# Last graph stage of a four-layer kernel: unrolled sweeps of unequal width, identity in the diagonal blocks, output rows on ScalarE

## What is computed

```
x = x + gnn0(layernorm(x))        # (adj != 0) @ (h @ W + b) / column sums
x = x + ffn0(layernorm(x))        # 8 experts, the best 2 of each row
x = x + gnn1(layernorm(x), adj)
x = x + ffn1(layernorm(x))

gnn1:  A_t = A + I;  deg = A_t.sum(1);  d = deg ** -0.5
       h = (A_t * d[:, None] * d[None, :]) @ x
       return relu(h @ W.T + b)

ffn1:  hot = x > 0.5 ; decode three one-hot groups of 16 columns (64.., 80.., 96..)
       shift the byte left or right; add 2.0 at a column of 128..143 and one of 144..159
       return x plus that, all 256 columns
```

## Time and profile before

| | us |
|---|---|
| median of 3 runs | 1169.84 |
| the profiled execution | 1168.45 |
| its span | 1166.6 |
| start of the last block | 823.06 |
| first adjacency matmul of the last block | 839.59 |
| last adjacency sum read (start of the last `high_sums`) | 1117.44 |

### The profile page before, as it was taken

How to read it: one execution, slowest core, us unless ns; L and a number is a source line. 1 busy time by engine, 2 the same in 40 slices (tenths; PEclk the granted TensorE clock), 3 DMA queues, 4 the chain that set the end, 5 groups by cost and what they waited for, 6 DMA issues and landing times. The chain is left out here.

```text
span 1166.6 us, 23614 instructions
## 1 busy us (share of the span) xinstructions
PE 985.5 (84%) x6868; PEld 641.1 (55%) x6869; DVE 576.4 (49%) x1661; ACT 388.6 (33%) x792; POOL 345.6 (30%) x359
## 2 busy tenths in 40 slices
PE   5559999999823899999999999995299997997941
PEld 1235544444401699899899899894044443443421
DVE  5633412136699466566566566562561106144077
ACT  3482867676694233233233233231121000000000
POOL 3310000024474254454455454453241001001011
PEclk9879999999955899999999999998599998998976
DMA  9466799899784133232333332232898775776201
GB/s 355 166 214 223 273 325 322 305 329 370 256 274 137 34 51 45 50 51 45 50 50 46 50 52 44 50 52 36 278 419 315 237 265 202 260 244 215 92 29 44
DMA packets 87008, 199.97 MB, mean 171 GB/s; under 512 B 12784, under 2 KB 47088, under 8 KB 86832
## 3 DMA queue, kind: packets, MB, share of 16 engines
q1 hardware_dynamic: 65136, 164.70, 40.5%
q0 software_dynamic: 17648, 30.49, 13.4%
q10 hardware_dynamic: 4176, 4.19, 1.0%
HBM read 176.41 MB, written 22.94 MB: 171 GB/s over the span
## 5 line engine op out<-in xcount | busy, mean ns | idle before, releaser
L955 PE MATMUL bank<-adj_f,feat 128*128 128x512 f16 x1024 | 243.5, 393 | 22.4 <-DMA adj_f<-in_adjT 22.4
L1586 PE MATMUL bank<-adj_g,feat 128*128 128x512 f16 x1024 | 241.0, 393 | 11.3 <-DMA adj_g<-in_adjT 11.3
L1231 ACT ACTIVATE act_f<-bank,b_sb 128x256 f32<-128x256 f32 x304 | 127.4, 470 | 291.9 <-PE bank L1176 291.9
L1176 PE MATMUL bank<-rT,experts 128*128 128x256 f16 x1824 | 208.5, 275 | 3.5 <-DVE rT L1244 3.5
L1197 PE MATMUL bank<-experts,act_h 128*128 x1824 | 205.3, 273 | 1.4 <-DVE y_f L1276 1.4
L1176 PEld LDWEIGHTS bank<-rT,experts 128*128 x1824 | 179.9, 99 | 26.1 <-issue 4.0
L1197 PEld LDWEIGHTS bank<-experts,act_h 128*128 128x128 f16 x1824 | 176.9, 98 | 21.5 <-issue 1.7
L955 PEld LDWEIGHTS bank<-adj_f,feat 128*128 128x128 f16 x1024 | 97.4, 97 | 149.6 <-issue 19.2
L1094 POOL DMA_INDIRECT x_rows<-y,token x76 | 122.1, 1607 | 194.1 <-DVE y L1283 166.4
L1586 PEld LDWEIGHTS bank<-adj_g,feat 128*128 x1024 | 99.1, 97 | 142.9 <-issue 19.4
L837 ACT ACTIVATE spent<-adj_f 128x1024 f16<-128x1024 f32 x128 | 135.1, 1055 | 39.4 <-DMA adj_f<-in_adjT 33.7
(11 more groups left out here) (257 smaller groups left out, 873.5 us busy)
## 6 DMA issues: line engine op xcount, KB each, us to landing
adj_f<-in_adjT SPq DMA_DIRECT2D x128, 512.0 KB, 5.9
adj_g<-in_adjT SPq DMA_DIRECT2D x128, 512.0 KB, 5.0
unit_f<-in_W SPq DMA_DIRECT2D x16, 512.0 KB, 7.1
stage<-in_W SPq DMA_DIRECT2D x12, 512.0 KB, 7.4
x_ring<-in_x POOLq DMA_DIRECT2D x16, 256.0 KB, 7.4
x_rows<-agg SPq DMA_DIRECT2D x4, 1024.0 KB, 10.6
x_sb<-x_rows SPq DMA_DIRECT2D x4, 1024.0 KB, 9.3
agg<-in_x ACTq DMA_DIRECT2D x3, 1024.0 KB, 13.7
```

What stands on the lines that cost most here:

```text
L955: last = pe.matmul(mine(s)[ib * DC + c][:, :], feat0[:, j, h, c * P:(c + 1) * P], adj_0[j % RING][:, ib * HALF_SWEEP:(ib + 1) * HALF_SWEEP ...
L1176: last = pe.matmul(pb[2 + q][:, k * SLOT:(k + 1) * SLOT], w1_part(e * DC + (f // FQ * W2_UNIT0 + c), wh)[:, (f % FQ) * P:(f % FQ + 1) * P] ...
L1231: last = a.activation(act_f[q][:, k, :], pb[2 + q][:, k * SLOT:(k + 1) * SLOT], ACT.Gelu, bias=b1_sb[:, ds(e * FC + (2 * q + k), 1)], scal ...
L1586: last = pe.matmul(mine(s)[ib * DC + c][:, :], feat[:, ds(jg * RING2 + b, 1), h, c * P:(c + 1) * P].rearrange("p a d -> p (a d)"), adj_1[b ...
```

## The change

It rewrites the last block, and adds four transfers to SP's queue in the experts block.

- The output rows are taken in five groups: 8, 8, 8, 4 and 4 row tiles (`GROUPS`), so two sweeps are 512 columns wide. Of those, a tile has 4 matmuls and its load is 256 KB in pieces of 2 KB.
- All loops of the block are unrolled.
- The sums open with `start=` at the first tile. `open_sums`, `add_self` and `eye` are gone. The identity is put into the adjacency tile itself: POOL multiplies the 128 x 128 diagonal block by `grow` (1, and 255 on the diagonal) and adds `ident`, so a diagonal 0 becomes 1 and a 1 becomes 256 (f16 upper half 3.75, twice FLAG).
- `rows_out` of the sweep before stand after tiles 3, 4, 5 ... of a sweep (`ROWS_FROM`).
- The first four adjacency tiles are loaded in the experts block, once DVE has split the last expert weights. The others alternate with the pieces of x, which are now 2, 6, 8, 8 and 8 tiles (`PIECES`).
- The output is made on ACT: `x * (rstd + 1) - mean * rstd` (`make_rows`). DVE makes z for 112 columns alone, and POOL's `add_rest` is gone. The norm's last step writes in place (one copy fewer). Statistics are taken tile by tile in each group.

```
-    w = Region(WORK_AT, X_AT)
+    adj_early = [Region(LATE_AT + k * 4096, W_AT)(f"adj_early{k}", [P, SWEEP], F32) for k in range(EARLY)]
+    GROUPS = ((0, 8), (8, 8), (16, 8), (24, 4), (28, 4))
+    ROWS_FROM = 3
 # experts block, sync
+            sp.wait_ge(sem("w2_parts"), UNITS - W2_UNIT0)
+            for j in range(EARLY):
+                sp.dma_start(adj_early[j][:, :], adj_v[j, :, 0:SWEEP]).then_inc(sem(f"adj_g_full{j}"), 16)
 # last block, sync
-            for g in range(NG):
-                sp.dma_start(x_sb[:, g * G:(g + 1) * G, :], ...)
-            for s in range(NS):
-                with sp.Fori(0, NJG2) as jg:
-                    for b in range(RING2):
-                        sp.wait_ge(sem("adj_g_used"), jg * RING2 + (s * NT + b + 1))
-                        sp.dma_start(adj_g[b][:, :], ...)
+            load_x2(0)
+            for g in range(1, len(PIECES)):
+                load_x2(g)
+                if g < 4:
+                    for j in range(g * 4, g * 4 + 4):
+                        load_tile(0, j)
+            for s in range(len(GROUPS)):
+                for j in range(16 if s == 0 else 0, NT):
+                    load_tile(s, j)
 # gpsimd
-            def add_rest(g):
-                pool.wait_ge(sem("z_ready"), g + 1)
-                for cols in (slice(0, OUTPUT_LO), slice(OUTPUT_LO + 32, D)):
-                    rest = x_sb[:, g * G:(g + 1) * G, cols]
-                    pool.tensor_tensor(rest, rest, z[:, :, cols], ALU.add).then_inc(sem("rest_added"), 1)
+            def add_self(s, t):
+                k = t - GROUPS[s][0]
+                square_block = adj_g[slot_of(s, t)][:, k * P:(k + 1) * P]
+                pool.wait_ge(sem(f"adj_g_full{slot_of(s, t)}"), loads_of(s, t))
+                pool.tensor_tensor(square_block, square_block, grow[:, :], ALU.mult).then_inc(sem("self_scaled"), 1)
+                pool.wait_ge(sem("self_scaled"), t + 1)
+                pool.tensor_tensor(square_block, square_block, ident[:, :], ALU.add).then_inc(sem("self_added"), 1)
+            for n in range(NT):
+                if own(0, n):
+                    add_self(0, n)
+                pool.wait_ge(sem("feat_hi_ready"), n + 1)
+                pool.tensor_tensor(feat[:, n, 1, :], scaled[:, n % 2, :], feat[:, n, 0, :], ALU.subtract)
+            for s in range(1, len(GROUPS)):
+                at, tiles = GROUPS[s]
+                for t in range(at, at + tiles):
+                    add_self(s, t)
+                store(s - 1)
 # vector, finish_rows
-                    st.did(v.tensor_scalar(z[:, b, :], x_sb[:, n + b, :], ...))
+                st.link(v.tensor_scalar(factor[:, part], rstd[:, part], 1.0, None, ALU.add))
+                v.scalar_tensor_tensor(out=shift[:, part], in0=mv[:, part, 0], scalar=-1.0, in1=rstd[:, part],
+                                       op0=ALU.mult, op1=ALU.mult).then_inc(sem("factors_ready"), 1)
+                    st.did(v.tensor_scalar(z[:, b, :], x_sb[:, n + b, 0:LOOKED], ...))
 # scalar
+            def make_rows(s):
+                n, tiles = GROUPS[s]
+                a.wait_ge(sem("factors_ready"), s + 1)
+                for b in range(tiles):
+                    a.activation(made[s % 2][:, b, :], x_sb[:, n + b, :], ACT.Identity, bias=shift[:, b:b + 1], scale=factor[:, b:b + 1])
 # tensor
-            def open_sums(s):
-            def add_self(s):
+                if own(s, j):
+                    pe.wait_ge(sem("self_added"), j + 1)
                 for h in range(2):
                     for c in range(DC):
-                        for ib in range(IB):
+                        for ib in range(halves(s)):
...
+                for j in range(NT):
+                    tile_sums(s, j)
+                    k = j - ROWS_FROM
+                    if s and 0 <= k < GROUPS[s - 1][1]:
+                        if k == 0:
+                            pe.wait_ge(sem("agg_lo_ready"), sums_before(s))
+                        if k >= 4:
+                            pe.wait_ge(sem("proj_ready"), GROUPS[s - 1][0] + k + 1)
+                        rows_out(s - 1, k)
+            for k in range(GROUPS[LAST_GROUP][1]):
+                rows_out(LAST_GROUP, k)
```

More of the change, by code:

```diff
@@ L19 @@
 RING2 = 16
-NJG2 = NT // RING2
+EARLY = 4
 HALF_SWEEP = 512
@@ L172, in tile_stats @@
         st.did(v.bn_stats(stats[:, b, :], row))
[L174 to L196, removed]
     def norm_root(a, tag, turn):
@@ L1317, in program @@
     proj = w("proj", [P, 2, D], F32)
-    z = w("z", [P, G, D], F32)
+    made = [w(f"made{i}", [P, G, D], F32) for i in range(2)]
+    factor = w("factor", [P, G], F32)
+    shift = w("shift", [P, G], F32)
+    LOOKED = 112
+    z = w("z", [P, G, LOOKED], F32)
     rank = w("rank", [P, 3 * 16], F32)
@@ L1337, in program, with halves, sums_before, slot_of @@
     out_v = out.rearrange("(n p) d -> p n d", p=P)
+    x2_v = x_rows[0:T, :].rearrange("(n p) d -> p n d", p=P)
     MARK, OP_SHL, OP_SHR, ALU_LO, OUTPUT_LO = 0, 39, 40, 64, 128
-    assert OT == G and NJG2 == 2 and OT == 4 * NJG2
-    OUT_AT = (4, 7, 10, 13)
+    assert ALU_LO + 48 == LOOKED
+    GROUPS = ((0, 8), (8, 8), (16, 8), (24, 4), (28, 4))
+    LAST_GROUP = len(GROUPS) - 1
+    assert sum(tiles for _, tiles in GROUPS) == NT
+    ROWS_FROM = 3
+    last_banks = [pb[k] for k in (2, 3, 6, 7)]
+    def halves(s):
+        return GROUPS[s][1] * P // HALF_SWEEP
+    def sums_before(s):
+        return sum(halves(i) * DC for i in range(s))
+    def slot_of(s, j):
+        return (s * NT + j) % RING2
+    def loads_of(s, j):
+        return ((s * NT + j) // RING2 + 1) * 16
+    def own(s, j):
+        return GROUPS[s][0] <= j < GROUPS[s][0] + GROUPS[s][1]
+    def bank_of(s, k):
+        return last_banks[k] if s == LAST_GROUP else other(s + 1)[k % 4]
     with nc.Block() as block:
@@ new lines, in finish_rows @@
+                hit = made[s % 2][:, part, OUTPUT_LO:OUTPUT_LO + 32]
+                v.wait_ge(sem("out_made"), n + tiles)
+                v.tensor_tensor(hit, hit, flat, ALU.add).then_inc(sem("out_ready"), 1)
+            st = Steps(v, sem("v_norm2"))
+            for g, (at, tiles) in enumerate(PIECES):
+                v.wait_ge(sem(f"x_loaded{g}"), 32)
+                st.wait()
+                st.did(v.memset(carry[:, 0:1], 0.0))
+                for b in range(tiles):
+                    st.did(v.bn_stats(stats[:, b, :], x_sb[:, at + b, :]))
+                factors(st, tiles, "n2_", g)
+                st.link(v.scalar_tensor_tensor(out=scale[:, 0:tiles], in0=rstd[:, 0:tiles], scalar=YS, in1=dinv[:, at:at + tiles],
@@ L1519, in _ @@
[L1519 to L1531 removed]
+            st = Steps(v, sem("v_norm3"))
@@ new lines, in _ @@
+            for s, (n, tiles) in enumerate(GROUPS):
+                low_sums(s)
+                for k in range(tiles + 2):
+                    if k < tiles:
+                        add_bias(n + k, bank_of(s, k))
+                    if 1 <= k <= tiles:
+                        add_relu(n + k - 1)
+                    if k >= 2:
+                        v.wait_ge(sem("x3_ready"), n + k - 2 + 1 + 2)
+                        tile_stats(v, st, k - 2, x_sb[:, n + k - 2, :])
+                finish_rows(s, st)
```

288 lines of the change are left out of this document (114 added, 174 removed).

## The result

The kernel after runs in 1107.64 us (median of 4 runs, 1106.47 to 1107.98), the kernel before beside it in 1170.11 (1168.48 to 1171.45). The ratio is 0.9468, 95% interval 0.9453 to 0.9483: 62.5 us less, where 1108.0 was forecast.

What follows compares the result with a forecast made beforehand. The last stage is a busy TensorE with two holes and an idle tail, where VectorE is late. From 1168.45, 8.8 + 23.9 + 28.5 - 0.5 = 60.7 gives 1107.8, forecast 1108; own range 1104 to 1111, 8 in 10 1101 to 1119.

Steps and rivals of the forecast that it cites:

- Loops: Unrolling the last block's loops saves nothing, as looped and unrolled matmuls both take 0.226 us.
- Start: Last block's opening: TensorE starts at about 831.5, 8.1 us earlier; sweep 0's sums are read at 892.6, 8.8 saved.
- The wait of 1.0 taken at tile 8: In sweep 0 TensorE waits for feature 8: 0.4 us came out, 1.0 was taken, bounds 0 and 5.
- Identity on GpSimd: GpSimd's identity pair and feature take 1.6 us a tile in sweep 0, hidden under TensorE's 1.81; later pairs hide too.
- Sweeps: Sweeps 1 to 4 of the last block: 192.1 us instead of 216.0, so 23.9 saved.
- Loads: Narrow sweeps' 256 KB adjacency loads, one each 0.90 us, cost 0; bounds 0 and 10 us.
- Third rival: Narrow adjacency loads go one after another at 2.9 us each: +120 us, 1228, slower than before; chance 0.02.
- Tail: From the read of the last sums to the span's end: 20.7 us instead of 49.2, 28.5 saved.
- The prediction's own sign: In the profile, 20 to 22 us from the last read of the sums to the end.
- Experts block: Early adjacency loads beside the first row gathers in the experts block cost 0.5 us; bounds 0 and 5.
- a boundary stays late, or the early loads cost: VectorE late after the first narrow sweep, up to 7.1 + 2.4, or early loads up to 5: 1115; chance 0.12.
- Features pace sweep 0: GpSimd's pairs slow the features and TensorE starves through x pieces 1 and 2: 3 to 6 us, 1112; chance 0.20.

Runs made afterwards that it cites:

- the second execution: The kernel after, unchanged, run once more beside two other kernels on one chip: 1108.54 us, ratio 0.9481.
- the last experiment: Kernel after with its last sweep split into two of 256 columns, 5 extra matmuls in the last wait, and x in pieces of 2, 6, 4, 4, 8, 8: 1103.12 us.

## Why the prediction was right

The mechanism held in each part, and every part came out within 1.0 us of its forecast. The median met the forecast to 0.4 us, which is closer than the terms deserve. Between the profiled executions the gain is 62.0 us where the sum had 60.7; that the sum began at an execution 1.7 us under its median, and that the one after lay 1.2 under its own, is luck.

- **Loops.** Forecast nothing. Right: 96 matmuls from 841.47 to the next start at 863.24, 0.2268 us each unrolled, where the loop had 0.226. The unrolling was not run by itself.
- **Start.** Forecast 831.5 for the first sum and 892.6 for the read; 831.62 and 892.45 came, in a block that began 0.4 us later (8.1 us from its start where 8.4 was forecast). The wait of 1.0 taken at tile 8 was there as lost time, in this execution as a longer cold start. The prediction did not divide the start among its edits; taken out one at a time the small first piece of x is worth 4.3 us and the early tiles 0.9.
- **Identity on GpSimd.** Right in size: a turn of 1.57 us, 1.0 us in sweep 0, none later.
- **Sweeps.** Forecast 192.1, measured 192.4. The swap on VectorE showed that waits and restarts were 19.0 us of the old 216.0; openings and identity less four more projections give the other 4.7 (5.2 by the prediction's terms). VectorE's slack in the first narrow sweep, 4 us in the prediction, was 5.7 (outputs done at 1047.5, read at 1053.2). The 0.3 us taken as left after the third sweep did not come: its rows follow the 16th matmul without a wait.
- **Loads.** Forecast 0, measured 0 down to 128 KB. The Trainium skill's "DMA: Bandwidth & Descriptors", Bandwidth, advises 1 MB or more for 75% of peak; no run here measures that share, and the kernel did not need it. The fit that the prediction quotes stands in another section of that page, Anatomy of one DMA — SWDGE (gpsimd) path, and is for transfers issued from GpSimd, while these are issued from SyncE. By it a 256 KB load would take an estimated 2.6 us; here one takes 3.2 us to land by the profile's row for `adj_g`, and one is used every 0.9 us, so several are under way. Third rival: out.
- **Tail.** Forecast 20.7, measured 19.7. Two terms were mis-sized: from the read to the aggregation 7.9 us instead of 8.6, because the rows ran at 2.4 GHz (8.5 in the second execution, where the clock fell), and the store with the end of the span 3.35 (1101.15 to 1104.5) instead of 4.0. From the aggregation to the last addition it was 0.3 more than the 8.1 taken, mostly `z` (1.1 us, 0.85 taken) and `hot` to `idx` (1.0, 0.85 taken). The prediction's own sign, 20 to 22 us, was missed on the short side. The gain of 29.5 splits, read from the kernel with the last sweep 1024 wide (tail 28.8): 9.1 width; 14.2 because the outputs of the sweep before no longer stand between the last sum and its rows (TensorE's wait falls from 17.36 to 3.21; 3.1 of this too is GpSimd's additions beside `hot` and `idx` of that sweep, since the wait was 14.28 without them); 3.1 for `hot` and `idx` of the last sweep; 0.7 for `z` on 112 columns; some 2.4 are left for the output on ScalarE, the store and the cold rows, not separated.
- **Experts block.** Forecast 0.5, nothing found (439.8 us from the first expert matmuls to the last block, before and after). The rival "a boundary stays late, or the early loads cost" falls with both halves.
- **Features pace sweep 0.** The rival was half right: the features do set sweep 0, but at one place, by 1 us and not by 3 to 6. With the third piece split, in the last experiment, 0.8 of it came back; an execution with the long cold start would not have shown that.

## What to carry to other kernels

Look at what stands ahead of the operation on which the busiest engine waits: here VectorE was in the last sweep's outputs when the low sums were due, which held TensorE for 7.1 us twice and cost 19 with the restarts. Swapping the two calls cured that in one run; in the kernel after VectorE gets the work earlier, and the waits are gone too. Work that must follow the last sum should be only that sum's own, and narrow: give each stage's outputs a place inside the next one, and halve the last one until the pace of its loads or its neighbours stops it (here 9.1 us off the tail for the first halving and 5.0 for the second, less 2.6 and 1.7 for the sweeps). An engine's wait at the end may be a symptom: removing 15 us of TensorE's wait there moved the end by nothing, since VectorE had the same work to do.

## What had not been expected of the hardware

- The same wait of 2.01 us, behind a long unbroken stretch at 2.4 GHz, kept the granted clock in four executions and lost it in two, 0.5 to 1.5 us into the rows behind it, at a cost of 0.6 to 1.1 us. A wait of 3.21 us kept it, both waits of 3.98 us (the kernel with GpSimd's additions late) lost it within the first microsecond of the rows, and in the wait of 12.11 us it was at 0.50 before the rows began.
- `idx`, on 24 columns, takes 0.18 us alone and 1.08 beside GpSimd; it ends within 0.04 us of GpSimd's addition. Such a hold-up shows in when an operation ends, not in its size.
